# Attention scores in split precision: the second pass over 64 rows in two halves of the TensorE array

## The reference, cut to what matters

```
# context: (16, 1601, 512); x: (16, 64, 512); 16 heads of 32 dimensions
q = layernorm(x) @ Wq + bq
kv = (context @ Wkv + bkv).reshape(B, 1601, 16, 32, 2);  k = kv[..., 0];  v = kv[..., 1]
scores = einsum('bhid,bhjd->bhij', q, k) * 32 ** -0.5
attn = softmax(scores, axis=-1)
x = x + einsum('bhij,bhjd->bhid', attn, v) @ Wout + bout
x = x + linear_attention(layernorm(x))
x = x + experts(layernorm(x))      # 8 experts, the best 2 of each row, inner size 1024
```

## Time and profile before

| | |
|---|---|
| median of three runs | 2389.8 us |
| profiled execution, its own time | 2389.21 us |
| its span | 2387.5 us |
| TensorE matmul busy (PE) | 2290.2 us, 96% |
| TensorE weight load busy (PEld) | 2027.0 us, 85% |
| VectorE (DVE) | 1254.6 us, 53% |
| ScalarE (ACT) | 1084.2 us, 45% |
| GpSimd (POOL) | 1128.0 us, 47% |
| mean granted TensorE clock | 0.984 |
| matmuls of the scores (L982) | 1024, 218.6 us of the PE time |

### The profile page before, as it was taken

The page is one execution under the profiler, slowest core; times in us unless marked ns, Lnnn a source line. Parts: engine busy times, 40 slices in busy tenths (PEclk is TensorE's granted clock), DMA queues, the critical chain, the costliest instruction groups (busy, mean ns, idle before and its releaser), DMA issues. The chain is left out here.

```text
span 2387.5 us, 41227 instructions
## 1 busy us (share of the span) xinstructions
PE 2290.2 (96%) x14545; PEld 2027.0 (85%) x14545; DVE 1254.6 (53%) x2143; ACT 1084.2 (45%) x1865; POOL 1128.0 (47%) x488
## 2 busy tenths in 40 slices
PE   8999999999999999999999999999987995899997
PEld 6798989899888989898998899898975885798886
DVE  3155555555555555555555555455566456556642
ACT  3254544444444445454454444454535322445442
POOL 1255555555555555555555555555565103334224
PEclk9999999999999999999999999999998997999998
DMA  4312111112121211111121212111131014656533
GB/s 157 104 47 57 43 50 43 51 47 63 31 78 32 69 51 43 50 43 51 47 62 35 74 34 67 51 43 49 43 113 38 20 54 158 182 179 201 183 118 81
DMA packets 146082, 175.51 MB, mean 74 GB/s; under 512 B 82112, under 2 KB 105536, under 8 KB 145856
## 3 DMA queue, kind: packets, MB, share of 16 engines
q1 hardware_dynamic: 136960, 147.11, 20.7%
q10 hardware_dynamic: 4608, 16.78, 2.2%
q0 software_dynamic: 4288, 8.67, 1.7%
HBM read 134.85 MB, written 37.65 MB: 72 GB/s over the span
## 5 line engine op out<-in xcount | busy, mean ns | idle before, releaser
L500 POOL TENSOR_TENSOR k_parts<-k_t,k_parts 64x1602 fp32r<-64x1602 f32 x128 | 426.1, 3329 | 447.6 <-DVE k_parts L592 447.5
L968 PE MATMUL ps_kv<-ctx_hi,wk_hi 128*128 128x256 f32 (+1 forms) x1536 | 462.1, 301 | 8.2 <-DVE ctx_lo L789 7.4
L968 PE MATMUL ps_kv<-ctx_hi,wk_lo 128*128 128x256 f32 (+1 forms) x1536 | 441.4, 287 | 0.0
L656 DVE TENSOR_TENSOR probs_t<-ps_pt,probs_t 128x512 fp32r<-128x512 f32 x376 | 208.1, 553 | 440.9 <-ACT probs_t L838 438.6
L968 PE MATMUL ps_kv<-ctx_lo,wk_hi 128*128 128x256 f32 (+1 forms) x1536 | 439.7, 286 | 0.0
L514 POOL TENSOR_TENSOR v_parts<-v,v_parts 128x832 fp32r<-128x832 f32 x120 | 267.3, 2228 | 321.3 <-ACT v_parts L856 320.0
L968 PE MATMUL ps_kv<-wv_hi,ctx_hi 128*128 128x512 f32 (+1 forms) x832 | 342.8, 412 | 1.8 <-DVE wv_lo L759 1.8
L826 ACT ACTIVATE k_t<-ps_kv,bk_sb 128x256 f32<-128x256 f32 (+1 forms) x384 | 185.9, 484 | 312.5 <-PE ps_kv L968 307.9
L968 PE MATMUL ps_kv<-wv_hi,ctx_lo 128*128 128x512 f32 (+1 forms) x832 | 327.0, 393 | 0.0
L968 PE MATMUL ps_kv<-wv_lo,ctx_hi 128*128 128x512 f32 (+1 forms) x832 | 326.8, 393 | 0.0
L968 PEld LDWEIGHTS ps_kv<-ctx_hi,wk_hi 128*128 128x128 f32 x1536 | 292.3, 190 | 11.3 <-issue 8.6
(11 more groups left out here) (304 smaller groups left out, 3930.5 us busy)
## 6 DMA issues: line engine op xcount, KB each, us to landing
ctx_raw<-ctx_dram SPq DMA_DIRECT2D x81, 512.0 KB, 3.8
w_raw<-w_dram SPq DMA_DIRECT2D x64, 512.0 KB, 4.2
rows_in<-zeros SPq DMA_DIRECT2D x150, 128.0 KB, 3.3
w_raw<-w_dram ACTq DMA_DIRECT2D x32, 512.0 KB, 3.6
ctx_raw<-ctx_dram SPq DMA_DIRECT2D x16, 644.0 KB, 4.4
q_blocks<-q_parts SPq DMA_DIRECT2D x256, 32.0 KB, 1.9
rows<-rows_in SPq DMA_DIRECT2D x8, 768.0 KB, 4.8
q_parts<-probs_t SPq DMA_DIRECT2D x16, 256.0 KB, 2.0
```

What stands on the lines that cost most here:

```text
L500: nc.gpsimd.tensor_tensor(k_parts[64 - 64 * s:128 - 64 * s, :], k_t[par][64 * s:64 * s + 64, g, :], k_parts[64 * s:64 * s + 64, :].bitcast ...
L656: nc.vector.tensor_tensor(probs_t[0:m, j:j + k, 1, :], ps_turned[kv][g][0:m, 0:k, :], probs_t[0:m, j:j + k, 0, :].bitcast(F32), ALU.subtra ...
L968: last = nc.tensor.matmul(o, still, moving, start=(k == 0 and i == 0), stop=(k == DT - 1 and i == 2))
```

## The change

The first pass stays: four matmuls over 128 rows. The second pass becomes q_lo x k_hi alone; q_lo x k_lo is left out. For that, each matmul of it takes only the 64 rows that hold k_hi, of the queries and of the keys. The columns are cut at 768 (`HALF`): for the first 768 keys k_hi lies where it did (the lower rows for an even pair), for the other 834 keys k_hi and k_lo lie in swapped halves. So two of the four matmuls of the second pass take the lower 64 rows of the array and two the upper 64, in turns: columns 0 to 255 (bank 0), 1280 to 1601 (bank 3), 256 to 767 (bank 1), 768 to 1279 (bank 2). The first column in PSUM moves so that the cut falls on a bank's edge; the widths become 256, 512, 512 and 322.

For the swapped half the keys must lie in the other 64 rows of `k_t` already. The key weights in SBUF get 64 more columns ahead (a copy of the last 64), and the K units of chunks 3 to 5 take their 128 columns 64 earlier. Block g of those chunks then holds the dimensions 128g-64 to 128g+63. The key bias is loaded a second time in that layout, with three small DMAs. VectorE's and GpSimd's `split_k` become two instructions for a pair, of 768 and of 834 columns; the wait for the whole keys goes by the new blocks.

```
+        def halves(p):
+            low, high = slice(0, TWO), slice(TWO, P)
+            first, second = (low, high) if p % 2 == 0 else (high, low)
+            return [(first, second, slice(0, HALF), block_of(p, 0)), (second, first, slice(HALF, LC2), block_of(p, 1))]
...
+            sp.dma_start(bk_sb[TWO:P, 1, :], bk[0:TWO, :]).then_inc(bias_loaded, 16)
+            sp.dma_start(bk_sb[0:TWO, 1, 1:DT], bk[TWO:P, 0:DT - 1]).then_inc(bias_loaded, 16)
+            sp.dma_start(bk_sb[0:TWO, 1, 0:1], bk[TWO:P, DT - 1:DT], allow_slow_non_contiguous=True).then_inc(bias_loaded, 16)
...
-                nc.gpsimd.tensor_tensor(k_parts[64 - 64 * s:128 - 64 * s, :], k_t[par][64 * s:64 * s + 64, g, :],
-                                        k_parts[64 * s:64 * s + 64, :].bitcast(F32), ALU.subtract
-                                        ).then_inc(k_lo_done, 1)
+                for hi, lo, cols, g in halves(p):
+                    last = nc.gpsimd.tensor_tensor(k_parts[lo, cols], k_t[par][hi, g, cols], k_parts[hi, cols].bitcast(F32),
+                                                   ALU.subtract)
+                last.then_inc(k_lo_done, 1)
...
-                nc.vector.tensor_copy(k_parts[64 * s:64 * s + 64, :], k_t[par][64 * s:64 * s + 64, g, :]
-                                      ).then_inc(k_hi_done, 1)
+                for hi, lo, cols, g in halves(p):
+                    last = nc.vector.tensor_copy(k_parts[hi, cols], k_t[par][hi, g, cols])
+                last.then_inc(k_hi_done, 1)
...
-                        dims = slice(which * P, (which + 1) * P)
+                        dims = slice(which * P + (TWO if CW * c < HALF else 0), (which + 1) * P + (TWO if CW * c < HALF else 0))
...
-                for part in range(2):
-                    for c0, c1 in SC:
-                        last = nc.tensor.matmul(ps_s[:, c0:c1], q_blocks[half][:, p % 4, part, :],
-                                                k_parts[:, c0 - S0:c1 - S0], start=(part == 0), stop=(part == 1))
+                for c0, c1 in SC:
+                    nc.tensor.matmul(ps_s[:, c0:c1], q_blocks[half][:, p % 4, 0, :], k_parts[:, c0 - S0:c1 - S0],
+                                     start=True, stop=False)
+                one, two = halves(p)
+                for i, (hi, lo, cols, g) in ((0, one), (3, two), (1, one), (2, two)):
+                    c0, c1 = SC[i]
+                    last = nc.tensor.matmul(ps_s[:, c0:c1], q_blocks[half][hi, p % 4, 1, :], k_parts[hi, c0 - S0:c1 - S0],
+                                            start=False, stop=True)
```

More of the change, by code:

```diff
@@ L38 @@
 TAIL = LC - (JT - 1) * P
+HALF = CW * CHUNKS // 2
+TWO = 2 * HD
 E, INTER = 8, 1024
@@ L120, with block_of @@
 START_LAST_OF_CHUNK = [max(n for n, u in enumerate(START) if u[1] == c) for c in range(CHUNKS)]
-START_K_WHOLE = [START.index(("K", LAST, p // 2)) for p in range(PAIRS)]
+def block_of(p, half):
+    return p // 2 if half == 0 else (p + 1) // 2 % DT
+START_K_WHOLE = [max(START.index(("K", LAST, block_of(p, 1))), START.index(("K", LAST // 2, block_of(p, 0))))
+                 for p in range(PAIRS)]
 FIRST_SCORES = NU - 3
-K_WHOLE = [UNITS.index(("K", CHUNKS - 1, p // 2)) for p in range(PAIRS)]
+K_WHOLE = [UNITS.index(("K", CHUNKS - 1, block_of(p, 1))) for p in range(PAIRS)]
 def pair_of_unit(n):
@@ L199, in sem @@
             return mem.enter_context(nc.semaphore(name))
-        wk_hi = sb("wk_hi", [P, DT, D], F32R)
-        wk_lo = sb("wk_lo", [P, DT, D], F32R)
+        wk_hi = sb("wk_hi", [P, DT, TWO + D], F32R)
+        wk_lo = sb("wk_lo", [P, DT, TWO + D], F32R)
         wv_hi = sb("wv_hi", [P, DT, D], F32R)
@@ L214, in cross_attention @@
         bq_sb = sb("bq_sb", [P, DT])
-        bk_sb = sb("bk_sb", [P, DT])
+        bk_sb = sb("bk_sb", [P, 2, DT])
         bv_sb = sb("bv_sb", [P, DT])
@@ L294, in cross_attention @@
         rows_flat = rows_in.rearrange("n d -> (n d)").rearrange("(k p c) -> k p c", p=P, c=ZERO_W)
-        S0 = (4 * BANK - LC2) // 2 // 2 * 2
+        S0 = 2 * BANK - HALF
         SC = [(max(c * BANK, S0), min((c + 1) * BANK, S0 + LC2)) for c in range(4)]
@@ L492, in split_k @@
             def split_k(b, par, p, chunks):
-                s, g = p % 2, p // 2
                 pool.wait_ge(k_hi_done, PAIRS * b + p + 1)
@@ L583, in split_k @@
             def split_k(b, par, p):
[L585 to L588, removed]
+                whole = START_K_WHOLE if isinstance(b, int) and b == 0 else K_WHOLE
+                dve.wait_ge(kv_copied, NU * b + whole[p] + 1)
                 n = PAIRS * b + p
@@ L753, in rest_of_keys @@
                 dve.wait_ge(w_hi_done, g + 1)
-                nc.vector.tensor_tensor(wk_lo[:, :, dims], wk_raw[:, :, dims], wk_hi[:, :, dims].bitcast(F32), ALU.subtract
+                if g == DT - 1:
+                    nc.vector.tensor_tensor(wk_lo[:, :, 0:TWO], wk_raw[:, :, D - TWO:D], wk_hi[:, :, 0:TWO].bitcast(F32),
+                                            ALU.subtract)
+                at = slice(TWO + g * P, TWO + (g + 1) * P)
+                nc.vector.tensor_tensor(wk_lo[:, :, at], wk_raw[:, :, dims], wk_hi[:, :, at].bitcast(F32), ALU.subtract
                                         ).then_inc(w_lo_done, 1)
@@ L797, in _ @@
             split_ctx(0, 3)
-            dve.wait_ge(bias_loaded, 48)
+            dve.wait_ge(bias_loaded, 96)
             for n in range(NQ):
@@ L826, in copy_unit @@
                     nc.scalar.activation(k_t[par][:, which, CW * c:CW * c + w], ps_kv[bank][:, 0:w], ACT.Identity,
-                                         bias=bk_sb[:, which:which + 1]).then_inc(kv_copied, 1)
+                                         bias=bk_sb[:, CW * c // HALF, which:which + 1]).then_inc(kv_copied, 1)
                 else:
@@ L911, in _ @@
                 act.wait_ge(wk_loaded[g], 16)
-                nc.scalar.copy(wk_hi[:, :, dims], wk_raw[:, :, dims]).then_inc(w_hi_done, 1)
+                if g == DT - 1:
+                    nc.scalar.copy(wk_hi[:, :, 0:TWO], wk_raw[:, :, D - TWO:D])
+                nc.scalar.copy(wk_hi[:, :, TWO + g * P:TWO + (g + 1) * P], wk_raw[:, :, dims]).then_inc(w_hi_done, 1)
             act.wait_ge(zeroed, 5)
-            act.wait_ge(bias_loaded, 48)
+            act.wait_ge(bias_loaded, 96)
             for kind, k in start_steps():
```

2 lines of the change are left out of this document (1 added, 1 removed).

## The result

| | before | after |
|---|---|---|
| median (12 runs of each) | 2390.37 us | 2394.61 us (2391.42 to 2399.16) |
| ratio, 95% interval | | 1.0017, 1.0010 to 1.0025 |
| profiled execution, span | 2389.21, 2387.5 us | 2397.84, 2396.1 us |
| mean granted clock | 0.984 | 0.980 |

The change costs 4.2 us, 0.18%: inside the forecast range and just under the 0.2% that was called no change, but the interval excludes zero. The profiled execution of after is 3.2 us longer than its median. A part of the 4.2 us can be the clock: the twelve executions of after show a mean granted clock of 0.9816, and 51 further ones of before, beside the experiments and on three chips, 0.9824. But it isn't all of it. Where the clock is 0.982 in both, the medians are 2392.75 (5 executions of after) and 2390.19 us (21 of before).

The account below looks back on a forecast made before the run. Not TensorE but the chain of ScalarE's copy and VectorE's rest was taken to bound each pair (1.65 us). Terms 0 + 0 + 0 + 0.6 on 2389.2, plus 0.6 for the median, gave 2390.4 us; range 2386.5 to 2397.

Parts of the forecast that it names:

- What bounds: Each pair: copy and rest before the turn of group 3 set 1.65 us; scores are off that path, gain 0.
- The second pass: Scores on TensorE: overlapping halves save 0.35 us per pair, mode changes cost 0.20 and 0.09; earliest turn 1.53 to 1.48.
- the sister case: Matmuls with 64 output rows in either half: sixteen took 1.62 us, not 1.95, so halves overlap in part.
- The price of the mode: TensorE switching into 64 rows and out again, twice per pair: 0.09 + 0.11 = 0.20 us a change.
- VectorE and GpSimd: One more split instruction each per pair, fixed 0.15 and at most 0.73 us, covered before the next scores: cost 0.
- The start: Three more SyncE loads delay the value weights; first V unit starts 0.55 us later: +0.6 us, at most 1.5.
- The last batch: Earlier scores' end gives 1.0 us, the copy's fixed part costs 0.9: taken as 0, bounds -1 and +1.
- rival 4: VectorE's 3 us pauses at loop turns shift as its body grows: 3 to 6 us either way; 3 in 100 beyond range.
- The sum: Whole kernel: 0 + 0 + 0 + 0.6 on 2389.2 gives 2389.8; median 0.6 above that, so 2390.4 us.
- Rivals 1, 2 and 3: Scores: halves serial, 2414 us, 9 in 100; dearer mode change, 2400 to 2419, 5; TensorE the bound, 2348 to 2362, 3.

Follow-up runs that it names:

- 3: Kernel before without the scores' second pass (q_lo x k left out): 2390.39 us, ratio 1.0005.
- 2: Kernel before with the second pass over 64 rows, all four matmuls in one half of the array: 2410.17 us, ratio 1.0087.
- 5: Kernel before with the turn of group 3 moved behind the first three matmuls of the next unit: 2368.46 us, ratio 0.9906.
- 6: Changed kernel with the turn of group 3 moved behind the first three matmuls of the next unit: 2376.02 us, ratio 0.9938.
- experiment 10: Changed kernel with the turn of group 3 moved behind the next unit's first three matmuls, second pass over 128 rows again: 2367.42 us, ratio 0.9914.
- 8: Kernel before with key copies and rests split into 768 and 834 columns everywhere but in the last batch: 2388.72 us, ratio 0.9998.
- 1: Changed kernel, layout kept, with the second pass over all 128 rows again: 2393.49 us, ratio 1.0015.
- 4: Changed kernel with the three added bias loads issued behind the query weights, with their own semaphore and wait: 2400.78 us, ratio 1.0052.
- 7: Kernel before with key copies and rests split into 768 and 834 columns in the last batch alone: 2390.42 us, ratio 1.0004.

## Why the prediction was right, point by point

**What bounds.** Right, and shown from four sides: the change of -0.14 us in the scores (after), of -0.72 (3) and of +0.20 (2), and the wait filled (5). The first three have the same threshold, 1.65 us; below it nothing happens, above it each hundredth counts in 120 pairs. That TensorE was busy 96% said nothing on it, since records overlap.

**The second pass.** The steps were: 1.69 to become about 1.55, measured 1.55; earliest turn 1.53 to 1.48, measured 1.53 (5) and 1.48 (6). Overlap, taken from the sister case of 64 output rows, held for 64 rows of the contraction. The price of the mode can now be taken apart. Into it: 0.09 until the first start (0.90 against the 0.81 of experiment 10) and 0.08 behind it, as the first two matmuls stand 0.22 us ahead of the next two (1011.07, 1011.29) where 322 columns are worth 0.147; 0.17 in all, I had 0.20. Out of it: the last two start 0.26 into the pass, and the next matmul comes at 0.58, 0.32 later for 512 columns that are worth 0.23; 0.09, as I had, and 0.10 for its own weights. The sentence that TensorE would gain nothing if it were the bound (0.35 less, 2 x 0.20 more, that is +0.05) is what 6 against 10 measured: +0.04.

**VectorE and GpSimd.** In the loop cost 0, as forecast: the steady pairs kept their length (after, 8). At the first pair the term was wrong, see the start. The fixed parts: VectorE's pair of copies takes 1.16 us against 0.99, 0.17 where I had 0.15, and GpSimd's

```profile
L522 POOL TENSOR_TENSOR k_parts<-k_t,k_parts 64x834 fp32r<-64x834 f32 x128 | 232.8, 1818 | 7.5
L522 POOL TENSOR_TENSOR k_parts<-k_t,k_parts 64x768 fp32r<-64x768 f32 x128 | 216.2, 1689 | 449.7 <-DVE k_parts L613 449.6
```

is 1.818 + 1.689 = 3.51 us against 3.33: 0.18 more, not the 0.73 of the bound. (That bound compared 64 rows with 128 rows; they are not on one line.)

**The start.** The size came out (+0.6 forecast, +0.8 measured), but by luck, as the way was wrong. The value weights were issued at 6.95 and not 4.91, later even than the 6.41 that I had, and ScalarE still began on them earlier than before:

```profile
6.95 0.43 SPq L474 DMA_DIRECT2D probs_both<-wv_dram  x1
...
12.99 1.89 ACT L945 CAST wv_hi<-probs_both 128x2048 fp32r<-128x2048 f32 x1
...
17.26 0.50 PE L995 MATMUL ps_kv<-wv_hi,ctx_hi 128*128 128x512 f32 x1 [1.85 <-DVE wv_lo L784]
```

The first V unit started 0.29 us earlier than before, not 0.55 later. What was overlooked stands at the other end of the start. The first scores wait for the rest of the first pair's keys, and nothing covers it: in all twelve traces they start 0.10 us behind the end of GpSimd's instruction. So the second instruction on VectorE and on GpSimd is paid here in full. Before, and then after:

```profile
102.75 0.99 DVE L592 CAST k_parts<-k_t 64x1602 fp32r<-64x1602 f32 x1 [11.40 <-ACT k_t L826]
...
106.95 3.62 POOL L500 TENSOR_TENSOR k_parts<-k_t,k_parts 64x1602 fp32r<-64x1602 f32 x1
...
110.67 1.72 PE L982 MATMUL ps_s<-k_parts,q_blocks 128*128 128x290 f32 x8 [1.23 <-issue]
```

```profile
103.03 1.16 DVE L613 CAST k_parts<-k_t 64x768 fp32r<-64x768 f32 x2 [11.40 <-ACT k_t L851]
...
107.52 3.84 POOL L522 TENSOR_TENSOR k_parts<-k_t,k_parts 64x768 fp32r<-64x768 f32 x2
...
111.46 0.97 PE L1008 MATMUL ps_s<-k_parts,q_blocks 128*128 128x256 f32 x4 [1.74 <-issue]
```

From VectorE's copy to the scores it is 7.92 us before and 8.43 after, 0.51 more. All five traces with the layout of after (after, 1, 4, 6, 10) have 8.42 or 8.43, the split in the halves of before (8) has 8.13, and the others have 7.91 or 7.92. The other 0.28 us arise ahead of that. Whether they are the loads' is not shown: the same place moves by -0.43 (4) to +0.25 (7) in the kernels that have no load there, and by +0.28 to +0.36 (after, 1, 10) and +1.29 (6) in those that have. They are not shown to be the clock's either. From 18.8 to 22.0 us the granted clock was 0.50 in after and 1.00 in before:

```profile
18.80:22.00 3.20, 3.20 (x9) 2.52 (x8) 2.70 (x6) 0.43 (x1) 1.91 (x1) 0.50 1.05 394
```

That put TensorE 1.28 us behind at 23 us, but by 28 us it was 0.28 behind, as before had stood still for 0.76 us there:

```profile
26.94 0.39 PE L968 MATMUL ps_kv<-ctx_hi,wk_hi 128*128 128x256 f32 x1 [0.76 <-ACT k_t L826]
```

**The last batch.** 0 forecast, bounds -1 to +1, and the trace shows +3.7. Two jumps make nearly all of it, +1.7 and +1.5, and both lie at stretches at 1.2 GHz; what is left is +0.5, inside the bounds:

```profile
1763.00:1769.80 6.80, 5.77 (x21) 4.43 (x22) 4.30 (x8) 1.99 (x4) 4.17 (x3) 0.50 1.07 376
1790.30:1797.10 6.80, 5.78 (x23) 5.26 (x24) 5.99 (x13) 2.33 (x4) 4.54 (x4) 0.50 0.00 0
```

In before the first is at 1.00 throughout

```profile
1762.00:1769.00 7.00, 6.58 (x35) 4.93 (x36) 5.64 (x11) 4.09 (x8) 5.46 (x3) 1.00 1.08 374
```

and the second has only 3.4 us of it. No term of mine had the clock in it, though the 0.92 of the earlier trace rows showed that it counts there. But the first stretch is not the change's. All eleven other traces have one that begins within 2 us of the same scores (pair 122), 3, 5 and 7, in the layout of before, among them, and 8, which has the last batch of before. It is the profiled execution of before that is the exception: its mean clock is 0.984, which 6 of 51 further executions of before show; the others have 0.980 to 0.983. So most of the +3.7 compares two executions and says little of the two kernels.

**The loop's pauses** (rival 4). They moved, by little: +1.1 us over the seams, against the 2 to 3 either way that my range held. The second pause of VectorE (o_t, 9.3 us in six) is in all five traces with the layout of after and in none of the others. Experiment 4 shows that they can be worth 9 us for a line that isn't in the loop.

**The sum.** 0.8 + 1.1 + 3.7 is 5.6 in the profiled execution, and its tail adds 2.9, part of it at lower clock (0.980 in all against 0.984); the medians differ by 4.2. Of these, 0.8 of the start, 1.1 of the seams and 0.5 of the last batch have a place in the trace, though the last two are read from a single execution of each kernel; where the rest of the 4.2 lies stays open. The forecast of 2390.4 was thus right in its main part, that the pairs keep their length, and too low in its small parts. The range's upper end was 0.7 us above what its own terms give (0.9 + 1 + 4 over 2390.4 is 2396.3); the measured 2394.6 lies under both. Rivals 1, 2 and 3 are refuted by the pair's timeline: the 64-row matmuls overlap, the turn is 0.05 behind the rest, and the pair is not shorter.

## What to carry to other kernels

Before valuing TensorE's work in a place, find the wait behind it and the chain that ends it, and write down the threshold (here 1.65 us): work below it is free in both directions, and the busy share doesn't show it. Then look for the one place where that cover is missing (here the first pair). What helped was to give TensorE something in the wait, an edit of a few lines for 20 us, where halving the scores gave none; only behind that is less work worth something. Packing two halves of the array has to win back two changes of mode, so for a pass of 1602 columns it doesn't pay (0.35 us saved, and 0.04 more than that spent). By these figures, as an estimate, a longer run of narrow matmuls between two changes would; none was run.

## What was not expected of the hardware

- The pauses with nothing awaited at the loop's seams changed with code outside the loop: with three loads and a wait moved in the start, ScalarE got a second pause of 1.3 to 1.5 us at each of the six, and three stretches at 1.2 GHz followed (experiment 4: 9 us). Whether it is the place of the code was not tested.
- A second GpSimd instruction over 64 rows costs 0.18 us, 3.51 against 3.33 us, as a mean of 128 pairs; in the last batch single pairs vary more than that (3.02 to 3.60 before, 3.25 to 3.81 after).
- The two matmuls of a pair of halves start 4 to 31 ns apart (in the pair shown, 1011.067 and 1011.071; 1011.291 and 1011.322), and each record is as long as one over 128 rows; only the distance of the pairs shows the gain:

```profile
L1008 PE MATMUL ps_s<-k_parts,q_blocks x420: 305/379/401, 309.7 to 1732.4; 128*128 128x512 f32 x70, 128*128 128x256 f32 x35, 128*128 128x322 f32 x35
L1013 PE MATMUL ps_s<-k_parts,q_blocks x420: 381/392/417, 310.6 to 1732.9; 64*128 64x512 f32 x70, 64*128 64x256 f32 x35, 64*128 64x322 f32 x35
```
